# A four-layer image network on one core: rows padded to a half of the array, the middle convolution tile on TensorE, the second projection in two column tiles

## The chip, the cores and the metric

The kernel runs on one core of a Trainium2 chip. The metric is the device time in microseconds (us) from start to end of the program; lower is better. All work is in float32 but for two feed-forward layers in fp8.

## What is computed

Thirty-two images of 56 x 56 pixels and 24 channels pass through two convolution blocks, a linear attention with a feed-forward layer, and a Fourier mixing layer with another one. The convolution block is the part that the change is about:

```
rw  = sigmoid(mean(x) @ Wr + br)                    # routing weights of each image
h   = x . (sum_e rw_e Wpw_e) + bias                 # 24 -> 96 channels, per image
h   = relu(bn1(h))
h   = sum_e rw_e * depthwise3x3(h, Wdw_e)           # per image and channel
h   = relu(bn2(h))
h   = h . (sum_e rw_e Wpwl_e) + bias                # 96 -> 24 channels, per image
x   = bn3(h) + x
...
t = t + attention(ln(t));  t = t + ffn_fp8(ln(t))
t = t + ifft(relu(diag * fft(relu(bn(ln(t) @ w1))))) @ w2;  t = t + ffn_fp8(ln(t))
```

## The kernel before

**Tiling.** Four images go together in a group (the code calls it a quad), eight groups in all. A group's state `T` has 4 x 24 = 96 rows (partitions), row 24 i + c for channel c of image i, and 3136 columns (pixels). Three such tiles take turns, so up to three groups are under way. The 4 x 96 = 384 hidden channels of a convolution make NT = 3 tiles of 128 rows: tile 0 is image 0 and a third of image 1, tile 1 the rest of image 1 and two thirds of image 2, tile 2 the rest. The weights of the four images stand in one block-diagonal matrix: `Wk1` (96 rows x 384 columns) and `Wk2` (three times 128 rows x 96 columns). A picture is cut into NS = 4 strips of 14 rows.

**A convolution layer.** For each strip and each hidden tile, TensorE makes the hidden values in two pieces of seven or eight picture rows (`hidden`, line 647; 392 or 448 columns) in one PSUM bank, and ScalarE rectifies each piece into `H1` (line 1015) before TensorE may write the next. The nine taps of tiles 0 and 1 are VectorE's (`taps`, line 1347), eight operations of 784 columns on `acc`, with the centre tap on ScalarE (line 1023). The taps of the last tile, `TJ` = 2, are TensorE's (line 666): 36 matmuls with diagonal weights, in four tiles of 64 x 64. ScalarE rectifies both kinds (lines 1046, 1052). `conv_out` is the second projection: for tiles 0 and 1, four matmuls of 128 rows by 96 columns, two in each of two PSUM banks (line 681), then for the last tile four of 64 rows by 96 columns (line 687). VectorE adds the result to `T` (line 1363). A float32 matmul stands in the trace as two records, each with its own weight load.

**Other stages.** A *middle* stream (m in the tables; PSUM banks 3 and 4) does two layer norms, the attention and the first feed-forward layer; a *back* stream (b; banks 5 to 7) does two layer norms, the Fourier layer and the second feed-forward layer. In a layer norm, line 711 centres 448 columns with a full-array matmul and line 702 sums the squares in four tiles of 32 columns. Lines 622, 747, 924 and 946 are transposes. The Fourier layer's first matmuls (line 856) read `Y`, a view of `arena`, whose row 96 holds ones for the bias; GpSimd fills it, and two zero pads, for each group (line 604).

**The order.** Each engine runs four streams, c (convolution up to the taps), d (`conv_end`), m and b, merged in the order of a table of numbers, `TURNS`: "c7 m1" is seven steps of c and one of m. Within a stream the groups follow each other. Engines meet only through semaphores.

## Time and profile before

| | us |
|---|---|
| median of 3 runs | 2727.1 |
| lowest and highest | 2726.68, 2732.29 |
| the profiled execution | 2732.07 |
| its span, first to last instruction | 2730.1 |

The profile is of one execution. A busy time is the union of an engine's instructions; matmuls overlap in it, so a duration of one record is longer than its share of the stream, and the step from start to start of what follows is the better measure. PE is TensorE, PEld its weight loads, DVE VectorE, ACT ScalarE, POOL GpSimd. The mean granted clock of TensorE was 0.88 of full speed, that is, it stood at 2.4 GHz for most of the time and at 1.2 GHz for the rest.

### The profile page before, as it was taken

Reading aid. Unit: us, or ns where it says so; the run is one execution under the profiler, and the core shown is the slowest. Engines: PE = TensorE matmul, PEld = TensorE weight load, DVE = VectorE, ACT = ScalarE, POOL = GpSimd, SP = SyncE. Lnnn points to the kernel's source line nnn. Section 1 sums busy time; section 2 is a strip of 40 time slices with the busy share of each in tenths; the row PEclk is TensorE's granted clock in tenths of the full one; section 3 lists DMA queues with packets and bytes.
Section 4 is the critical chain, followed back from the end, with each engine's and each line's share of the span. In section 5 each row is a group of like instructions: output and inputs, shape, how many; then the busy total and the mean of one; then the engine's idle time right before and its main releaser. Section 6 shows DMA issues by size and latency. Waiting matters only on the chain.

```text
span 2730.1 us, 49134 instructions
## 1 busy us (share of the span) xinstructions
PE 2370.9 (87%) x19776; PEld 1324.3 (49%) x19776; DVE 1955.3 (72%) x3878; ACT 1680.7 (62%) x2818; POOL 69.3 (3%) x119
## 2 busy tenths in 40 slices
PE   3867979999898988989898989989899998987866
PEld 1323434564346634664346634665355634663562
DVE  4766778588775977678785978578786887755243
ACT  2324455756756666666756658666776667756644
POOL 1000000000000000000000000000000000000000
PEclk9878888989888988989898998989899998977865
DMA  4001000000001000010001000010000000000000
GB/s 131 1 1 18 1 1 1 11 10 1 18 1 19 2 1 19 2 19 1 13 6 20 1 1 19 2 19 1 1 19 9 2 1 19 2 1 1 19 1 18
DMA packets 108592, 29.43 MB, mean 11 GB/s; under 512 B 104144, under 2 KB 104272, under 8 KB 107984
## 3 DMA queue, kind: packets, MB, share of 16 engines
q1 hardware_dynamic: 108368, 26.29, 4.8%
q8 instruction: 159, 2.61, 0.4%
q14 instruction: 65, 0.53, 0.1%
HBM read 16.64 MB, written 9.63 MB: 10 GB/s over the span
## 4 chain that ended last, share of the span: by engine, by line
PE 61%; DVE 19%; ACT 14%; issue 4%; SPq 1%; DMA 0%; ACTq 0%; POOL 0%; DVEq 0%; POOLq 0%
PE P L666 13%; PE P L647 9%; PE P L711 6%; PE P L681 6%; DVE acc L1347 5%; PE P L856 4%; PE P L687 3%; PE P L702 2%; PE P L869 2%; PE P L897 2%; ACT H L1015 2%; PE P L911 2%; PE P L784 2%; DVE SQ L1482 2%; PE P L725 2%
## 5 line engine op out<-in xcount | busy, mean ns | idle before, releaser
L1347 DVE SCALAR_TENSOR_TENSOR acc<-H,Dm,acc 128x784 f32<-128x784 f32 x1024 | 989.6, 1026 | 189.6 <-ACT acc L1023 189.2
L647 PE MATMUL P<-T,Wk 96*128 96x448 f32 (+1 forms) x768 | 409.3, 618 | 68.4 <-ACT H L1015 51.6
L666 PE MATMUL P<-H,diag 64*64 64x392 f32 x4608 | 409.9, 506 | 5.6 <-DVE T L1363 4.8
L1015 ACT ACTIVATE H<-P,biasA 128x448 f32<-128x448 f32 (+1 forms) x384 | 238.6, 621 | 234.9 <-PE P L647 188.4
L666 PEld LDWEIGHTS P<-H,diag 64*64 64x64 f32 x4608 | 174.3, 137 | 223.3 <-issue 211.3
L711 PE MATMUL P<-T,pack_b 96*96 96x448 f32 x448 | 229.2, 600 | 12.0 <-DVE T L1363 5.8
L647 PEld LDWEIGHTS P<-T,Wk 96*128 96x128 f32 x768 | 137.1, 208 | 180.0 <-ACT H L1015 109.6
L681 PE MATMUL P<-acc,Wk 128*96 128x392 f32 x512 | 202.1, 542 | 25.3 <-ACT acc L1052 25.2
L1046 ACT ACTIVATE acc<-P,biasT 128x392 f32<-128x392 f32 x128 | 68.7, 583 | 228.7 <-PE P L666 228.7
L881 PE MATMUL P<-pack_b,arena 128*96 128x112 f32 x928 | 134.4, 302 | 41.1 <-DVE roots L1482 22.6
L881 PEld LDWEIGHTS P<-pack_b,arena 128*96 128x96 f32 x928 | 116.2, 193 | 72.9 <-DVE roots L1482 32.0
L681 PEld LDWEIGHTS P<-acc,Wk 128*96 128x96 f32 x512 | 87.6, 178 | 126.2 <-issue 125.7
L1023 ACT ACTIVATE acc<-H,Dm 128x784 f32<-128x784 f32 x128 | 121.4, 949 | 27.4 <-PE P L687 25.7
L1482 DVE SCALAR_TENSOR_TENSOR SQ<-P,fneg,arena 96x224 f32<-96x224 f32 x64 | 27.6, 431 | 133.6 <-ACT arena L1156 133.2
L1363 DVE SCALAR_TENSOR_TENSOR T<-P,bias,T 96x392 f32<-96x392 f32 x128 | 75.8, 618 | 65.3 <-PE P L687 61.3
L1052 ACT ACTIVATE acc<-acc,biasA 128x784 f32<-128x784 f32 x128 | 119.0, 950 | 5.2 <-DVE acc L1347 5.1
L856 PEld LDWEIGHTS P<-pack_b,arena 97*64 97x64 f32 x1792 | 111.9, 216 | 18.4 <-issue 10.4
L1116 ACT ACTIVATE mid<-P 128x448 f16<-128x448 f32 x168 | 91.8, 546 | 44.9 <-PE P L823 44.7
L856 PE MATMUL P<-pack_b,arena 97*64 97x96 f32 x1792 | 116.4, 292 | 1.7 <-DVE arena L1387 1.6
L1132 ACT ACTIVATE arena<-P 128x384 f32<-128x384 f32 x112 | 93.9, 854 | 35.9 <-PE P L856 29.5
L1156 ACT ACTIVATE arena<-P,pack_b 96x224 f32<-96x224 f32 (+1 forms) x128 | 59.7, 516 | 70.3 <-DVE arena L1466 68.1
L687 PE MATMUL P<-acc,Wk 64*96 64x392 f32 x256 | 100.3, 510 | 0.0
(186 smaller groups left out, 3886.3 us busy)
## 6 DMA issues: line engine op xcount, KB each, us to landing
xin<-in_x SPq DMA_DIRECT2D x224, 42.0 KB, 2.3
out_y<-arena SPq DMA_DIRECT2D x8, 1176.0 KB, 5.7
pack_b<-in_pack_b SPq DMA_DIRECT2D x1, 3804.0 KB, 17.3
arena<-in_pack_s SPq DMA_DIRECT2D x1, 1444.0 KB, 8.5
pack_a<-in_pack_a SPq DMA_DIRECT2D x1, 1084.0 KB, 5.3
pack_i<-in_pack_i SPq DMA_DIRECT2D x1, 318.0 KB, 3.1
arena<-in_pack_k SPq DMA_DIRECT2D x1, 192.0 KB, 3.2
```

The costliest lines, as they stand in the source:

```text
L647: pe.matmul(conv_rows(slice(0, 128), H1B, m), Wk1[:, 128 * (u % NT):128 * (u % NT + 1)], image_rows(T[q % 3], a + r0, m), start=True, stop ...
L666: last = pe.matmul(conv_rows(slice(64 * h, 64 * (h + 1)), CVB + r, HH), diag[64 * r:64 * (r + 1), tap, :], H1[64 * r:64 * (r + 1), slot(s, ...
L681: pe.matmul(conv_rows(slice(0, R), CVB + h, HH), Wk2[:, j, :], image_rows(acc[:, (NT * s + j) % N2, :], HH * h, HH), start=(j == 0), stop= ...
L687: last = pe.matmul(conv_rows(slice(0, R), CVB + h, HH), w, image_rows(acc[rows, (NT * s + TJ) % N2, :], HH * r, HH), start=False, stop=(r ...
L711: pe.matmul(P[0:R, norm.cen[c % NC], 0:CK], par["cen"][0:R, :], T[q % 3][:, CK * c:CK * (c + 1)], start=True, stop=True).then_inc(norm.cen ...
L856: last = pe.matmul(P[64 * j:64 * (j + 1), B0 + g % BN, R * s:R * (s + 1)], Y_x[:, 4 * g + s, :], par["fw1"][0:R + 1, R * j:R * (j + 1)], s ...
L881: last = pe.matmul(P[0:R, B0 + g % BN, o:o + 2 * HW], Y2[:, s // 2, s % 2, :], par["f"][:, s // 2, :], start=True, stop=True)
L1015: act.activation(H1[:, slot(s, j), o + r0:o + r0 + m, 1:1 + HW], conv_rows(slice(0, 128), H1B, m), ACT.Relu, bias=biasA[:, j, 1:2]).then_i ...
L1023: act.activation(acc[:, u % N2, :].rearrange("p (r w) -> p r w", w=HW), H1[:, slot(s, j), 1:1 + SR, 1:1 + HW], ACT.Copy, scale=Dm[:, j, CE ...
L1052: act.activation(a, a, ACT.Relu, bias=biasA[:, j, 0:1]).then_inc(h2_ready.sem, 1)
L1132: act.activation(Hf[:, :, 4 * g:4 * g + 4].rearrange("p c x -> p x c"), P[:, B0 + g % BN, 0:4 * R].rearrange("p (s n) -> p s n", s=4), ACT ...
L1347: ins = ve.scalar_tensor_tensor(a, H1[:, slot(s, j), r:r + SR, c:c + HW], Dm[:, j, tap:tap + 1], a, ALU.mult, ALU.add)
```

## The change

- Rows: 16 spare rows come first in `T` and all that is laid out like it, so R is 112 (`RC` is the old 96). Images 0 and 1 have rows 16 to 63, images 2 and 3 rows 64 to 111. Transposes to and from this layout, and results in it, are 112 rows or columns wide.
- `TJ` is 1: TensorE's taps take the middle hidden tile; VectorE's are tiles 0 and 2.
- `hidden` (now line 680): the pieces come in the order tile 0, 2, 1. Tile 0 needs only images 0 and 1 and contracts over rows 0 to 63; tile 2 contracts over rows 64 to 111; tile 1 over all 112.
- `conv_out`: first the middle tile's four matmuls (line 716), then, for each bank, tile 0 into output rows 0 to 63 and tile 2 into rows 64 to 111 (line 720), 128 rows by 64 and by 48 columns. They are as many as before: eight.
- GpSimd: the row of ones becomes a fill of 32 rows by 3136 columns (rows 96 to 127 of the arena), made before the third layer norm writes row 96 and up; ScalarE's first copy there waits for it. One more small fill comes before attention, and TensorE and ScalarE wait for both.
- The middle stream's first matmul of a group waits for VectorE's last addition of the group before (`added`) instead of ScalarE's copy (`out_half`).
- The turned tile of the Fourier layer is made in seven groups of four instead of six of up to five.
- One more VectorE operation in the setup, other constants, and new tables `TURNS`.

```diff
--- before.py
+++ after.py
@@ -27,7 +27,9 @@
 TOK = HW * HW
 CH = 24
 QI = 4
-R = QI * CH
+RC = QI * CH
+PAD = 64 - 2 * CH
+R = PAD + RC
...
-        Wk2 = sb("Wk2", [128, NT, R])
+        Wk2p = sb("Wk2", [128, PAD + NT * RC])
+        Wk2 = Wk2p[:, PAD:].rearrange("p (j n) -> p j n", j=NT)
...
-            return 4 if j == TJ else 2 * (s % 2) + j
+            return 4 if j == TJ else 2 * (s % 2) + j // 2
+
+        pieces = ((0, 0), (0, 1), (2, 0), (2, 1), (TJ, 0), (TJ, 1))
+        NP = len(pieces)
+
+        def piece_rows(s, k):
+
+            a, n, o = strip_rows(s)
+            return (a, 8, o) if k == 0 else (a + 8, n - 8, o + 8)
...
                 hold(pool_e, normM.y_ready, normM.y_ready.at(q, NCK))
-                pool_e.memset(YT[:, :, R:R + 1], 1.0).then_inc(ones_ready.sem, 1)
+                pool_e.memset(YT[:, :, RC:RC + 1], 1.0).then_inc(ones_ready.sem, 1)
+                pool_e.wait_ge(ones_ready.sem, ones_ready.at(q, 1))
+                pool_e.memset(bdw[2][:, 0:PAD], 0.0).then_inc(ones_ready.sem, 1)
 
             def back(q):
                 yield
 
                 if q == 0:
                     pool_e.wait_ge(setup_late.sem, 1)
+                hold(pool_e, normB.y_ready, normB.y_ready.at(q, 0))
+                pool_e.memset(arena[96:128, reg1:reg1 + TOK], 1.0).then_inc(fpads_set.sem, 1)
+                pool_e.wait_ge(fpads_set.sem, fpads_set.at(q, 1))
+                yield
                 hold(pool_e, out_stored, out_stored.at(q, 16))
-                for n, (dst, value) in enumerate(((Y[0:R, TOK:], 0.0), (Y[R:R + 1, :], 1.0), (Hf[:, :, HW:64], 0.0))):
-                    pool_e.memset(dst, value).then_inc(fpads_set.sem, 1)
-                    pool_e.wait_ge(fpads_set.sem, fpads_set.at(q, n + 1))
+                for n, dst in enumerate((arena[:, reg1 + TOK:reg1 + 64 * HW], Hf[:, :, HW:64])):
+                    pool_e.memset(dst, 0.0).then_inc(fpads_set.sem, 1)
+                    pool_e.wait_ge(fpads_set.sem, fpads_set.at(q, n + 2))
...
-                for u in range(NU):
-                    a, n, _ = strip_rows(u // NT)
-                    for k, (r0, m) in enumerate(((0, 8), (8, n - 8))):
+                for s in range(NS):
+                    for e, (j, k) in enumerate(pieces):
+                        a, n, _ = piece_rows(s, k)
                         yield
-                        if u == 0 and k == 0:
+                        if s == 0 and e == 0:
                             pe.wait_ge(cw_ready.sem, cw_ready.at(q, L + 1))
                         else:
-                            pe.wait_ge(h1_ready.sem, h1_ready.at(q, 2 * (L * NU + u) + k))
-                        pe.matmul(conv_rows(slice(0, 128), H1B, m), Wk1[:, 128 * (u % NT):128 * (u % NT + 1)],
-                                  image_rows(T[q % 3], a + r0, m), start=True, stop=True).then_inc(h1_psum.sem, 1)
+                            pe.wait_ge(h1_ready.sem, h1_ready.at(q, NP * (L * NS + s) + e))
+                        rows = {0: slice(0, 64), TJ: slice(0, R), 2: slice(64, R)}[j]
+                        pe.matmul(conv_rows(slice(0, 128), H1B, n), Wk1[rows, 128 * j:128 * (j + 1)],
+                                  image_rows(T[q % 3][rows, :], a, n), start=True, stop=True).then_inc(h1_psum.sem, 1)
...
-                pe.wait_ge(h2_ready.sem, h2_ready.at(q, L * NV + TJ * (s + 1)))
-                for j in range(TJ):
-                    for h in range(2):
-                        pe.matmul(conv_rows(slice(0, R), CVB + h, HH), Wk2[:, j, :], image_rows(acc[:, (NT * s + j) % N2, :], HH * h, HH),
-                                  start=(j == 0), stop=False)
+                pe.wait_ge(h2_ready.sem, h2_ready.at(q, L * NV + 2 * (s + 1)))
                 for r in range(2):
                     for h in range(2):
                         rows = slice(64 * h, 64 * (h + 1))
-                        w = Wk2[rows, TJ, :] if r == h else Wk2t[rows, :]
-                        last = pe.matmul(conv_rows(slice(0, R), CVB + h, HH), w,
-                                         image_rows(acc[rows, (NT * s + TJ) % N2, :], HH * r, HH), start=False, stop=(r == 1))
-                        if r == 1:
-                            last.then_inc(cv_psum.sem, 1)
+                        w = Wk2p[rows, TJ * RC:TJ * RC + R] if r == h else Wk2t[rows, :]
+                        pe.matmul(conv_rows(slice(0, R), CVB + h, HH), w,
+                                  image_rows(acc[rows, (NT * s + TJ) % N2, :], HH * r, HH), start=(r == 0), stop=False)
+                for h in range(2):
+                    for j, out_rows, w in ((0, slice(0, 64), Wk2p[:, 0:64]), (2, slice(64, R), Wk2[:, 2, 2 * CH:RC])):
+                        last = pe.matmul(conv_rows(out_rows, CVB + h, HH), w, image_rows(acc[:, (NT * s + j) % N2, :], HH * h, HH),
+                                         start=False, stop=True)
+                    last.then_inc(cv_psum.sem, 1)
...
-                    pe.wait_ge(ffns[0].out_half.sem, ffns[0].out_half.at(q, 0))
+                    pe.wait_ge(ffns[0].added.sem, ffns[0].added.at(q, 0))
...
-                    for xx in range(5 * g, min(5 * g + 5, HW // 2)):
-                        o = R * (xx % 5)
-                        last = pe.transpose(P[0:4 * K1, B0 + g % BN, o:o + R], Wf2[:, xx, :], par["ident"][0:R, 0:R])
+                    for xx in range(4 * g, 4 * g + 4):
+                        o = R * (xx % 4)
+                        last = pe.transpose(P[0:4 * K1, BB[g % BN], o:o + R], Wf2[:, xx, :], par["ident"][0:R, 0:R])
...
+                    if n == 2 and c == 0:
+                        act.wait_ge(fpads_set.sem, fpads_set.at(q, 1))
...
-        "d7 b1 c10 m1 c10 m1 c6 b1 c4 m1 c6 b1 c4 m1 c6 b1 c4 m1 c6 b1 c4 m1 c6 b1 c4 m1 c6 b1 c4 m1 b1 "
+        "d7 b2 c11 m1 c10 m1 c5 b1 c4 b1 c1 m1 c5 b1 c4 b1 c2 m1 c4 b1 c4 b1 c2 m1 c4 b1 c4 b1 c2 m1 c4 b1 c4 "
```

Line numbers shift: 647 to 680, 666 to 699, 687 to 716, 681 to 720, 711 to 743, 702 to 734, 604 to 628 and 633.

TensorE around the second projection of the first strip of the fourth group. Lines 911 and 924 are steps of the Fourier layer, 666 the taps. Before:

```order
L711 MATMUL P<-T,pack_b 96x448
L702 MATMUL P<-mid,pack_b 32x112 x4
L911 MATMUL P<-pack_b,arena 96x112 x5
L681 MATMUL P<-acc,Wk 96x392 x4
L687 MATMUL P<-acc,Wk 96x392
L687 MATMUL P<-acc,Wk2t 96x392 x2
L687 MATMUL P<-acc,Wk 96x392
L711 MATMUL P<-T,pack_b 96x448
L702 MATMUL P<-mid,pack_b 32x112 x4
L924 MATMUL P<-pack_i,arena 116x96 x28
L647 MATMUL P<-T,Wk 128x448
L666 MATMUL P<-H,diag 64x392 x36
```

Now, at the same projection (757 spreads the deviations of a layer norm):

```order
L680 MATMUL P<-T,Wk 128x448
L757 MATMUL P<-thirdsm,selb 112x448 x2
L716 MATMUL P<-acc,Wk 112x392
L716 MATMUL P<-acc,Wk2t 112x392 x2
L716 MATMUL P<-acc,Wk 112x392
L720 MATMUL P<-acc,Wk 64x392
L720 MATMUL P<-acc,Wk 48x392
L720 MATMUL P<-acc,Wk 64x392
L720 MATMUL P<-acc,Wk 48x392
L680 MATMUL P<-T,Wk 128x448
```

The four matmuls over 128 rows moved behind the four over 64 rows and are 64 and 48 columns wide, and the neighbours are other steps: the convolution stands earlier against the other streams.

TensorE in the hidden pieces of the fourth group's second layer. Before (823 and 809 are feed-forward matmuls, 946 output transposes):

```order
L823 MATMUL P<-mid,w1q 128x448 x2
L647 MATMUL P<-T,Wk 128x448
L946 MATMUL P<-pack_i,T 112x96 x12
L647 MATMUL P<-T,Wk 128x392
L823 MATMUL P<-mid,w1q 128x448
L809 MATMUL P<-mid,w2q 96x448 x3
L946 MATMUL P<-pack_i,T 112x96 x4
L647 MATMUL P<-T,Wk 128x448
```

Now:

```order
L743 MATMUL P<-T,pack_b 112x448
L680 MATMUL P<-T,Wk 128x448
L734 MATMUL P<-SQ,pack_b 32x112 x4
L743 MATMUL P<-T,pack_b 112x448
L734 MATMUL P<-SQ,pack_b 32x112 x4
L680 MATMUL P<-T,Wk 128x392
L743 MATMUL P<-T,pack_b 112x448
L734 MATMUL P<-mid,pack_b 32x112 x4
L680 MATMUL P<-T,Wk 128x448
```

As before, single pieces stand between steps of other streams; those of tiles 0 and 2 now use 64 x 128 tiles of the array, while line 743 and the feed-forward matmuls use all of it.

GpSimd around the fills for the second group. 567 and 590 build the diagonals, 573 and 596 clear edge rows. Before:

```order
L567 TENSOR_TENSOR diag<-pack_i,Dm 128x576 [waits edge_rows_zero_tensor,conv_weights_ready]
L604 MEMSET arena 96x448 [waits diagonals_ready,out_stored]
L604 MEMSET arena 1x3584 [waits fourier_pads_set]
L604 MEMSET arena 128x96x8 [waits fourier_pads_set]
L573 MEMSET H 128x2x56 [waits fourier_pads_set,acc_ready]
```

Now:

```order
L628 MEMSET arena 32x3136 [waits diagonals_ready,normalised_ready_back]
L596 MEMSET H 128x2x56 [waits fourier_pads_set,acc_ready]
L596 MEMSET H 128x56 [waits edge_rows_zero,taps_in_psum]
L596 MEMSET H 128x2x56 [waits edge_rows_zero_tensor,acc_ready]
L596 MEMSET H 128x56 [waits edge_rows_zero,taps_in_psum]
L633 MEMSET arena 128x448 [waits edge_rows_zero_tensor,out_stored]
L633 MEMSET arena 128x96x8 [waits fourier_pads_set]
```

The long fill stands ahead of a layer's four edge clears, the pads behind them.

## Rows read from the trace of the kernel before

In a timeline the columns are start and length in us, engine, line, operation, output and inputs, form and number of records. A form like 96\*128 is rows by columns of the weights.

**Rows 1.** Page: span, busy time of engines, chain shares by engine
```profile
span 2730.1 us, 49134 instructions
...
PE 2370.9 (87%) x19776; PEld 1324.3 (49%) x19776; DVE 1955.3 (72%) x3878; ACT 1680.7 (62%) x2818; POOL 69.3 (3%) x119
...
PE 61%; DVE 19%; ACT 14%; issue 4%; SPq 1%; DMA 0%; ACTq 0%; POOL 0%; DVEq 0%; POOLq 0%
```

**Rows 2.** Busy us by engine, granted clock, in start, middle and end
```profile
core 0: us, PE busy (x) PEld busy (x) DVE busy (x) ACT busy (x) POOL busy (x), PEclk, DMA share, GB/s
0.00:400.00 400.00, 295.93 (x1589) 126.19 (x1589) 261.18 (x455) 155.03 (x253) 15.15 (x27) 0.87 0.11 26
400.00:2400.00 2000.00, 1830.00 (x16074) 1039.64 (x16072) 1550.68 (x3037) 1341.98 (x2248) 49.75 (x89) 0.91 0.05 8
2400.00:2731.00 331.00, 244.93 (x2115) 158.48 (x2115) 143.48 (x388) 183.65 (x317) 4.40 (x4) 0.69 0.03 8
```

**Rows 3.** Chain that ended last: shares of the span by line
```profile
by line: PE P L666 12.6%; PE P L647 9.0%; PE P L711 6.5%; PE P L681 5.6%; DVE acc L1347 5.4%; issue 4.5%; PE P L856 4.2%; PE P L687 2.6%; PE P L702 2.2%; PE P L869 2.1%; PE P L897 2.1%; ACT H L1015 1.8%; PE P L911 1.6%; PE P L784 1.5%; DVE 
```

**Rows 4.** Timeline, TensorE, one second projection: start, us, line, form, records
```profile
928.01 2.80 PE L681 MATMUL P<-acc,Wk 128*96 128x392 f32 x8
930.74 0.57 PE L687 MATMUL P<-acc,Wk 64*96 64x392 f32 x1
...
931.80 0.49 PE L687 MATMUL P<-acc,Wk2t 64*96 64x392 f32 x1
...
932.23 0.99 PE L711 MATMUL P<-T,pack_b 96*96 96x448 f32 x2
933.15 0.40 PE L702 MATMUL P<-mid,pack_b 96*32 96x112 f32 x8
933.48 2.74 PE L924 MATMUL P<-pack_i,arena 96*116 96x96 f32 x28
```

**Rows 5.** Timeline, TensorE: full tiles between 32-column tiles
```profile
954.26 1.67 PE L711 MATMUL P<-T,pack_b 96*96 96x448 f32 x4
955.85 0.40 PE L702 MATMUL P<-mid,pack_b 96*32 96x112 f32 x8
956.18 1.02 PE L647 MATMUL P<-T,Wk 96*128 96x448 f32 x2
957.13 0.40 PE L702 MATMUL P<-SQ,pack_b 96*32 96x112 f32 x8
```

**Rows 6.** Groups of instructions on TensorE: busy us, mean ns, idle before
```profile
L666 PE MATMUL P<-H,diag 64*64 64x392 f32 x4608 | 409.9, 506 | 5.6 <-DVE T L1363 4.8 <-ACT H L1015 0.8
L647 PE MATMUL P<-T,Wk 96*128 96x448 f32 x576 | 308.4, 619 | 51.9 <-ACT H L1015 35.6 <-DVE biasT L1328 15.6
...
L681 PE MATMUL P<-acc,Wk 128*96 128x392 f32 x512 | 202.1, 542 | 25.3 <-ACT acc L1052 25.2
...
L869 PE MATMUL P<-pack_b,arena 128*64 128x58 f32 x3072 | 93.9, 223 | 1.0 <-ACT arena L1132 0.9
...
L747 PE MATMUL P<-pack_i,mid 96*112 96x96 f32 x224 | 38.5, 311 | 6.3 <-ACT mid L1079 4.2 <-POOL mid L595 2.1
...
L924 PE MATMUL P<-pack_i,arena 96*116 96x96 f32 x224 | 22.1, 250 | 1.1 <-ACT arena L1174 1.1
```

**Rows 7.** Waits of line 647: us in total, times, longest
```profile
PEld P L647 <- ACT H L1015: 109.6, 105, 2.7
```

**Rows 8.** Timeline, line 856 in two column tiles: matmuls and weight loads
```profile
2028.18 1.04 PEld L856 LDWEIGHTS P<-pack_b,arena 97*64 97x64 f32 x16 [0.65 <-issue]
2028.18 1.20 PE L856 MATMUL P<-pack_b,arena 97*64 97x96 f32 x16
...
2029.31 1.02 PE L647 MATMUL P<-T,Wk 96*128 96x448 f32 x2
```

**Rows 9.** Line 681: shortest, median and longest record
```profile
L681 PE MATMUL P<-acc,Wk x512: 490/492/941, 75.9 to 2390.7; 128*96 128x392 f32 x171
```

**Rows 10.** Line 604, the fills on GpSimd
```profile
L604 POOL MEMSET arena<- x24: 467/742/3096, 34.5 to 2547.0; 96x448 f32 x8, 1x3584 f32 x8, 128x768 f32 x8
```

More of the change, by code:

```diff
@@ L732, in gram @@
                         y = YT[:, BPG * (g % 2) + s, :]
-                        last = pe.matmul(P[0:R + 1, 4, 0:R + 1], y, y, start=(g == 0 and s == 0),
+                        last = pe.matmul(P[0:RC + 1, MB[1], 0:RC + 1], y, y, start=(g == 0 and s == 0),
                                          stop=(g == NCK - 1 and s == BPG - 1))
@@ L1038, in rectify_taps @@
+                        relu1(s, e)
+                        if k == 1 and j != TJ:
+                            yield
+                            centre_tap(s, j, e)
             def rectify_taps(q, L, s):
@@ L1579, in _parameters, with below @@
 def _parameters(a):
-    row_c = np.arange(R) % CH
+    row_c = np.concatenate([np.zeros(PAD, int), np.arange(RC) % CH])
+    com_c = row_c[PAD:]
     hid = np.arange(NT * 128) % HID
     p = {}
+    def below(v, ahead=0):
+        return np.pad(v, ((PAD, 0), (ahead, 0)))
     def tiles(v):
```

301 lines of the change are left out of this document (157 added, 144 removed), and 214 rows, old and new, of the table TURNS.

## The prediction

> **What bounds the kernel now.** I read the engines' busy times first. TensorE is busy 87% of the span, VectorE 72%, ScalarE 62%, and the chain of work that ended last runs through TensorE for 61% of it [rows 1]. By stage: between 400 and 2400 us TensorE is busy 1830 of 2000 us; in the first 400 us it is idle 104 us and in the last 331 us 86 us, because there few groups of images overlap [rows 2]. So a term is worth its full price only in the middle. The chain by line then says how much of a line's time is on the path: line 681 has 5.6% and line 687 2.6%, together 224 us of 2730; line 647 has 9.0%, 246 us [rows 3].
>
> **The second projection (the gain).** Before, one projection of a strip is eight records of line 681 (four float matmuls, two records each) and eight of line 687. The first eight start at 928.01 and line 687 starts at 930.74: 2.73 us. Line 687 takes until the next line starts at 932.23: 1.49 us. Together 4.22 us [rows 4]. In 2.73 us the engine streams 8 records of 392 columns, 0.33 us each (2.64), and 0.09 us are left, just where the tiling changes from the full array to two row tiles. Line 687 streams four rounds of two records that start in pairs (4 x 0.33 = 1.32); 0.17 us remain: 0.08 for the first weight load, which nothing hides, and 0.09 for leaving the tiling.
>
> After, line 716 is the old line 687 with 112 output rows, and line 720 has four matmuls in two column tiles, 64 and 48 wide. If each pair runs together, line 720 streams four rounds: 1.32, plus 0.06 for the first load (64 columns against 96 for 0.08) and 0.09 for leaving. With the entry into row tiles (0.09, formerly inside the 2.73) the new projection costs 0.09 + 1.49 + 1.32 + 0.15 = 3.05 us; I take 3.04. It saves 1.18 us; there are 64 strips (8 groups x 2 layers x 4), so 75.5 us. These are rows at the full clock of 2.4 GHz; the mean record of line 681 is 542 ns against a median of 492 [rows 6, 9], so some ran at the half clock and I multiply by 1.10: **83 us**. Of the old 64 x 4.22 = 270 us, 224 were on the chain, 83%. The gain on the path is **69 us**.
>
> Do the column pairs run together? The trace has such tiles. Line 666 has four 64x64 tiles with 392 columns: 4608 records in 409.9 us, 0.089 us each against 0.33 alone, nearly four at once [rows 6]. Line 869, two column tiles of 58 columns, takes 0.031 us a record where 58/392 x 0.33 gives 0.049 alone [rows 6]. Line 856 is the row against: 16 records of 96 columns from 2028.18 to 2029.31, 1.13 us, where perfect pairs would need 0.65; but its weight loads alone are busy 1.04 us, so loads bound it [rows 8]. At 392 columns a record streams 0.33 us over a load of 0.06. I take full pairing; the other end is a loss, priced below.
>
> The Trainium skill speaks less hopefully: in "TensorE: Matmul & The Clock Gate", Part 3, its table of measured speedups gives three column tiles 2.38 times, not 3. An estimate with that page's 0.79 would stretch the 1.32 us to 1.67 and take about 20 us from the gain; line 666 here shows no such loss.
>
> **The hidden matmuls (the cost).** The outer tiles' pieces at line 680 now contract over rows 0 to 63 or 64 to 111, so they run in 64x128 tiles, between neighbours that mostly use the full array. They gain nothing by it: each writes the one hidden bank and waits for the piece before. What a change of tiling costs is in a quiet stretch: line 711 takes four records from 954.26 to 955.85, 1.59 us, of which 4 x 0.377 (448 columns) is 1.51 and 0.08 to 0.09 is the exit to the 32-column tiles; line 647, between two such groups, takes 0.95 us for two records where 0.75 would do: 0.09 to leave and 0.11 for a weight load that is not hidden behind the matmul before it [rows 5]. So a change costs 0.09 plus 0.08 to 0.11: 0.19 us. Counted over the whole order of TensorE with each line's tile, there are 832 changes before and 1173 after. 64 of the 341 more are inside the projection and paid above; 277 remain, 277 x 0.19 = 53 us, 58 with the same clock factor. Where TensorE waits for ScalarE anyway the entry is free: 105 of 384 loads of line 647 did [rows 7], 27%, and entries are half of the changes, so 13% off: 50 us. Line 647 streams 288 x 0.75 + 96 x 0.66 = 279 us and has 246 on the chain, 88%. The cost on the path is **44 us**; its bounds are 0 (no drain for this tile) and 58.
>
> The Trainium skill has this rule, "TensorEngine Tiling (Array Packing)", section Tiling Modes: changing the mode, not merely the tile, drains the array. It gives no price; the trace agrees, with 0.09 us.
>
> **Wider rows.** Three transposes stream 112 columns instead of 96. At lines 747 and 924 that is 448 records [rows 6] of 16 more columns: 16/392 x 0.33 = 13 ns, 6 us; the output transposes, by the same step, up to 3 more. Loads of 112 columns after a change of tiling are 13 ns longer, some 250 times: 3 us. Together 9 to 12, on the path **8 us**. ScalarE's copies of the turned tile go from six to seven for each group of images, behind other work except in the last group, 1 us.
>
> **GpSimd and waits.** The long fill moves: 1x3584 took 3.10 us [rows 10], now 32x3136, by length 2.7 us, in front of ScalarE's first centred copy of the third layer norm. It only has to wait for the fourth layer norm of the group before, and a whole feed-forward stage follows that; GpSimd is busy 69 us of 2730 [rows 1]. I count nothing. If it stands behind an edge clear that waits for VectorE, all 2.7 us show, 8 times, 22 us at most. The second small fill before attention delays TensorE's first transpose, which already waited for that fill (2.1 us in all [rows 6]): 8 x 0.17, 1 us. The middle stream's first matmul now waits for VectorE's last addition, one operation later: 0 to 1 us each, I take 1 in all. VectorE's taps, the largest share outside TensorE, keep their number and size.
>
> **The sum.** -69 + 44 + 8 + 1 + 1 + 1 = -14 us. The order of all engines is also a new one. Before, 164 us of TensorE's work, by the row durations, lay behind the last projection; now 208: the convolutions run ahead. They start earlier (the third group's transposes after 261 us of such work instead of 319), which fills part of the 104 us idle at the start and takes work to the end. I take -6 for it, with bounds of -55 (some 30% of the 190 us idle at both ends) and +30 (the 44 us more at the end, run at two thirds). Sum **-20 us** on the profiled execution's 2732.1, so 2712; the median of the runs shown is 5 us lower, so **2707 us**.
>
> **Rivals.**
> - The changes of tiling win (slower). The saved time is on the path only while TensorE is what ends last at the projection; the changes are paid in every stretch. If half of the 83 us is off the path (VectorE's taps or the single hidden bank set the pace) and the 58 us are paid in full, with 11 for widths and waits: -41 + 58 + 11 = +28, 2755. It decides once less than (50 + 11)/83 = 73% of the gain is on the path; the chain says 83%. 24%.
> - The new order wins more: -14 - 45 = -59, 2668. For it: 190 us of idle at both ends [rows 2]. Against it: no row says the new order fills them. 17%.
> - The 64x128 tiles drain nothing, so the change of the hidden pieces is free: -69 + 10 = -59, 2668. Against: line 687 paid 0.17 us in the same tile [rows 4]. 7%.
> - The change doesn't do what it says: column pairs run one after another. Line 720 then takes 2.64 and a projection 4.37: +10 us, and with 44 + 11 + 0: +65, 2792. Only line 856 speaks for it. 4%.
>
> **How the numbers follow.** My forecast has 48% and its own range is 2685 to 2730. The range reaches to both kinds of neighbour: 2648 to 2760. A measurement tells 0.2%, 5.5 us, from no change. Faster: 0.48 x 0.78 + 0.17 + 0.07 = 0.61. Same: 0.48 x 0.18 + 0.04 of the first rival = 0.13. Slower 0.26.
>
> **What would show it.** Line 720's records start in pairs 0.33 us apart and its eight take 1.4 to 1.5 us (right), or one by one for 2.7 (wrong). Line 680's pieces of 64 rows take 0.95 us and the line behind them starts 0.09 late. TensorE's time at lines 716 and 720 on the chain falls from 8.2% to 5.5 to 6% of the span. Line 647's share, 9.0%, rises to 10 to 11% at line 680. ScalarE shows no wait for GpSimd at the third layer norm. I am wrong if the chain's share of VectorE rises while TensorE's idle time between 400 and 2400 us, 170 us now, grows by more than 40 us.

## The result and the profile after

| | before | after |
|---|---|---|
| median | 2730.7 us | 2757.5 us |
| lowest and highest of 6 runs | 2726.7, 2732.5 | 2748.2, 2766.2 |
| the profiled span | 2730.1 | 2752.3 |

The ratio is 1.01 (95%: 1.0078 to 1.0122): the changed kernel is slower, by 27 us. The forecast was 2707 us, with 61% on faster. The sign was wrong; the time lies inside the range, near the 2755 of the first rival.

The page of the changed kernel, as [rows 1] (busy time and instructions of each engine, then the chain by engine):

```profile
span 2752.3 us, 49178 instructions
...
PE 2350.1 (85%) x19776; PEld 1284.7 (47%) x19776; DVE 1951.9 (71%) x3879; ACT 1679.9 (61%) x2826; POOL 70.1 (3%) x130
...
PE 62%; DVE 16%; ACT 14%; issue 5%; SPq 3%; DMA 1%; ACTq 0%; DVEq 0%
```

TensorE is busy 21 us less than before, yet the span is 22 us longer. The chain has a new part: SyncE's queue (SPq) with 3% where it had 1%, and DMA with 1% where it had 0%.

The same three stretches as [rows 2] (columns as there):

```profile
0.00:400.00 400.00, 287.24 (x1574) 120.06 (x1575) 264.13 (x453) 149.94 (x246) 15.47 (x31) 0.84 0.11 26
400.00:2400.00 2000.00, 1806.27 (x15494) 984.04 (x15494) 1524.87 (x2990) 1317.44 (x2215) 49.99 (x94) 0.90 0.04 8
2400.00:2753.00 353.00, 256.58 (x2713) 180.64 (x2711) 162.85 (x437) 212.55 (x366) 4.67 (x5) 0.79 0.03 8
```

TensorE's idle time is 113, 194 and 96 us, where it was 104, 170 and 86. In the middle 2000 us it gets through 15494 matmuls where it did 16074, and those missing turn up behind 2400 us (2713 against 2115, in a stretch 22 us longer).

The chain by line, as [rows 3] (680 was 647, 716 was 687, 720 was 681):

```profile
by line: PE P L699 12.4%; PE P L680 11.0%; PE P L743 6.0%; issue 4.6%; PE P L888 4.4%; PE P L716 4.3%; DVE acc L1381 4.1%; PE P L720 3.4%; PE P L901 2.8%; SPq L553 2.5%; PE P L734 1.9%; PE P L929 1.8%; ACT H L1047 1.8%; PE P L913 1.8%; DVE 
```

The hidden matmuls rose from 9.0% to 11.0%, as forecast. Lines 716 and 720 have 7.7%; 5.5 to 6 were forecast, 8.2 stood before. And line 553, SyncE's input load, has 2.5% of the chain, where all of SyncE's queue had 1% before.

One second projection of the changed kernel, TensorE's timeline (start, length, line, form, records), as [rows 4]:

```profile
566.96 1.02 PE L680 MATMUL P<-T,Wk 48*128 48x448 f32 x2
567.91 0.59 PE L757 MATMUL P<-thirdsm,selb 96*112 96x448 bf16 x2
568.42 0.58 PE L716 MATMUL P<-acc,Wk 64*112 64x392 f32 x1
...
569.93 1.53 PE L720 MATMUL P<-acc,Wk 128*64 128x392 f32 x8
571.39 1.01 PE L913 MATMUL P<-pack_b,arena 128*96 128x112 f32 x8
```

Line 716 takes 1.51 us from its start to that of line 720, and line 720's eight records 1.46: together 2.97, where the sum had 1.49 and 1.32 + 0.15. The column pairs stream two at a time, as forecast, and the 48-row piece of line 680 takes the 0.95 us that was forecast.

What was not forecast is before the first step of each group. Groups of TensorE's instructions at the input transposes (busy, mean ns, idle before and its releasers), before and then after:

```profile
L622 PE MATMUL P<-pack_i,xin 112*96 112x112 f32 x224 | 37.8, 321 | 27.3 <-DMA xin<-in_x 27.3
```
```profile
L655 PE MATMUL P<-pack_i,xin 112*112 112x112 f32 x224 | 41.6, 335 | 75.8 <-DMA xin<-in_x 75.8
```

TensorE waits 76 us for input data where it waited 27. The diff of the kernel has one line on this that the prediction did not look at:

```diff
                     n = q * NCK + g
                     if n >= XG:
-                        sp.wait_ge(in_tp.sem, n - XG + 1)
-                    o = RC * BPG * (n % XG)
+                        sp.wait_ge(in_tp.sem, n - XG + 2)
+                    o = PAD + RC * BPG * (n % XG)
```

The input buffer has `XG` = 4 slots for the seven blocks of a group. A transpose of 112 columns also reads the 16 columns ahead of its slot, which are the end of the slot before it. So a slot may be filled again only when the next slot has been read too, and the load waits for one block more. The loads of the next group's first four blocks are issued ahead of time; the fourth of them (block 3 of group q + 1) now waits until that group's own first block is transposed. SyncE works in order, and behind this load stand the store of group q - 2 and the other loads. SyncE's queue in the kernel before, and after:

```profile
736.37 0.33 SPq L536 DMA_DIRECT2D out_y<-arena  x1
850.03 15.46 SPq L531 DMA_DIRECT2D xin<-in_x  x28
1046.31 0.33 SPq L536 DMA_DIRECT2D out_y<-arena  x1
```
```profile
807.98 0.49 SPq L558 DMA_DIRECT2D out_y<-arena  x1
808.51 319.85 SPq L553 DMA_DIRECT2D xin<-in_x  x28
1128.40 0.52 SPq L558 DMA_DIRECT2D out_y<-arena  x1
```

Before, the store left at 1046 and the loads for the next group followed when slots came free. After, the store leaves at 1128, behind the last of 28 loads, which were begun at 808. What happens there, in the timeline of all engines (the number in brackets is the idle time before a record):

```profile
1125.85 1.33 PE L655 MATMUL P<-pack_i,xin 112*112 112x112 f32 x12
...
1126.44 1.91 SPq L553 DMA_DIRECT2D xin<-in_x  x4
...
1128.40 0.52 SPq L558 DMA_DIRECT2D out_y<-arena  x1
...
1128.96 14.02 SPq L553 DMA_DIRECT2D xin<-in_x  x22
...
1130.35 0.92 PE L655 MATMUL P<-pack_i,xin 112*112 112x112 f32 x4 [2.14 <-DMA xin<-in_x]
...
1135.47 1.00 PE L655 MATMUL P<-pack_i,xin 112*112 112x112 f32 x4 [4.19 <-DMA xin<-in_x]
```

The first transposes free the load (1126.44), the store goes out behind it, and the rest of the loads follow in single file while TensorE waits for each: 2.14 us, 4.19 us, at the head of a group on which all its other engines depend.

### The profile page after: what moved, and what is told of

The parts are those of the page before. It is cut to its first block, busy times and chain, and to the rows that moved or that the text cites. A ratio compares the mean times of both kernels' runs of the same rounds, so it can differ in the third digit from the quotient of the medians.

```text
span 2752.3 us, 49178 instructions
## 1 busy us (share of the span) xinstructions
PE 2350.1 (85%) x19776; PEld 1284.7 (47%) x19776; DVE 1951.9 (71%) x3879; ACT 1679.9 (61%) x2826; POOL 70.1 (3%) x130
## 4 chain that ended last, share of the span: by engine, by line
PE 62%; DVE 16%; ACT 14%; issue 5%; SPq 3%; DMA 1%; ACTq 0%; DVEq 0%
PE P L699 12%; PE P L680 11%; PE P L743 6%; PE P L888 4%; PE P L716 4%; DVE acc L1381 4%; PE P L720 3%; PE P L901 3%; SPq L553 2%; PE P L734 2%; PE P L929 2%; ACT H L1047 2%; PE P L913 2%; DVE SQ L1517 2%; PE P L757 2%
## 5 line engine op out<-in xcount | busy, mean ns | idle before, releaser
L680 PE MATMUL P<-T,Wk 64*128 64x448 f32 (+5 forms) x768 | 432.8, 648 | 72.8 <-ACT H L1047 46.0
L743 PE MATMUL P<-T,pack_b 112*112 112x448 f32 x448 | 237.2, 621 | 19.7 <-ACT mid L1094 10.3
L680 PEld LDWEIGHTS P<-T,Wk 64*128 64x128 f32 (+2 forms) x768 | 129.5, 208 | 224.2 <-ACT H L1047 119.7
L716 PE MATMUL P<-acc,Wk 64*112 64x392 f32 x256 | 132.9, 650 | 29.8 <-ACT acc L1083 29.7
L888 PEld LDWEIGHTS P<-pack_b,arena 113*64 113x64 f32 x1792 | 117.0, 216 | 41.6 <-issue 25.2
L716 PE MATMUL P<-acc,Wk2t 64*112 64x392 f32 x256 | 131.3, 653 | 0.0
L888 PE MATMUL P<-pack_b,arena 113*64 113x96 f32 x1792 | 126.9, 304 | 3.6 <-ACT arena L1165 2.7
L1397 DVE SCALAR_TENSOR_TENSOR T<-P,bias,T 112x392 f32<-112x392 f32 x128 | 78.6, 623 | 64.2 <-PE P L720 63.1
L743 PEld LDWEIGHTS P<-T,pack_b 112*112 112x112 f32 x448 | 69.3, 188 | 88.8 <-issue 71.4
L720 PE MATMUL P<-acc,Wk 128*64 128x392 f32 (+1 forms) x512 | 110.6, 558 | 0.0
L655 PE MATMUL P<-pack_i,xin 112*112 112x112 f32 x224 | 41.6, 335 | 75.8 <-DMA xin<-in_x 75.8
```

What stands on the lines that cost most here:

```text
L680: pe.matmul(conv_rows(slice(0, 128), H1B, n), Wk1[rows, 128 * j:128 * (j + 1)], image_rows(T[q % 3][rows, :], a, n), start=True, stop=True ...
L716: pe.matmul(conv_rows(slice(0, R), CVB + h, HH), w, image_rows(acc[rows, (NT * s + TJ) % N2, :], HH * r, HH), start=(r == 0), stop=False)
L720: last = pe.matmul(conv_rows(out_rows, CVB + h, HH), w, image_rows(acc[:, (NT * s + j) % N2, :], HH * h, HH), start=False, stop=True)
L743: pe.matmul(P[0:R, norm.cen[c % NC], 0:CK], par["cen"][0:R, :], T[q % 3][:, CK * c:CK * (c + 1)], start=True, stop=True).then_inc(norm.cen ...
L888: last = pe.matmul(P[64 * j:64 * (j + 1), BB[g % BN], RC * s:RC * (s + 1)], Y_x[:, 4 * g + s, :], par["fw1"][0:R + 1, RC * j:RC * (j + 1)] ...
```

## The experiments

Each ratio is to the kernel before, measured on the same chip, with its 95% interval. Medians of the kernel before were 2736.0, 2731.9 and 2730.6 us on the three chips, so differences of medians between kernels on different chips are good to some 5 us; where it matters the difference of the two ratios is given too, in us of the kernel before. With the intervals of both ratios such a difference is known to some 8 to 13 us. "Best" is the name, in the labels and here, of the kernel with both edits of the first three experiments.

**The input wait, taken away in the changed kernel.** Each slot gets 16 zero columns of its own, and the load waits as it did before.

```diff
-        xin = sb("xin", [BLK, PAD + XG * BPG * RC])
+        SL = PAD + BPG * RC
+        xin = sb("xin", [BLK, XG * SL])
...
-                        sp.wait_ge(in_tp.sem, n - XG + 2)
-                    o = PAD + RC * BPG * (n % XG)
+                        sp.wait_ge(in_tp.sem, n - XG + 1)
+                    o = PAD + SL * (n % XG)
...
-                        o = RC * (BPG * (n % XG) + s)
+                        o = SL * (n % XG) + RC * s
```

> The changed kernel, with 16 zero columns of its own in front of each of the four input slots, so that a slot may be loaded again as soon as its own transposes are done (the wait of the kernel before). In the changed kernel TensorE is idle 70 us before its input transposes (line 655), in the kernel before 21 us (line 622). Theory A (the stricter wait on the input slots is the missing cost): that idle time falls back to 15 to 30 us and the time by 35 to 50 us, to 2708 to 2722 us (before: 2731). Theory B (the changes of the array's tiling at the hidden matmuls are the whole of the slowdown, the input wait is covered by other slack): 2745 to 2758, and the idle time turns up at another line.

2735.3 us (10 runs, 2724.9 to 2744.5), ratio 1.0001 (0.998 to 1.0021): 22 us less than the changed kernel's 2757.5 (27 by the ratios), and no different from the kernel before. That is below theory B's range, and a smaller fall than theory A's 35 to 50: the wait is a cost, but not all of it. The input transposes now wait:

```profile
L656 PE MATMUL P<-pack_i,xin 112*112 112x112 f32 x224 | 38.3, 316 | 51.6 <-DMA xin<-in_x 51.1 <-ACT T L1029 0.4
```

So 24 of the 76 us went, and 22 to 27 us of the end with them. The other 24 us over the 27.3 of before stay, although the wait is the old one.

**The row tiles of the hidden matmuls, taken away.** All pieces contract over 112 rows with the full array (their weights are zero in the rows of images that the tile does not hold); the rest is the changed kernel. TensorE's order then has 900 changes of tiling, not 1173.

```diff
-                        rows = {0: slice(0, 64), TJ: slice(0, R), 2: slice(64, R)}[j]
-                        pe.matmul(conv_rows(slice(0, 128), H1B, n), Wk1[rows, 128 * j:128 * (j + 1)],
-                                  image_rows(T[q % 3][rows, :], a, n), start=True, stop=True).then_inc(h1_psum.sem, 1)
+                        pe.matmul(conv_rows(slice(0, 128), H1B, n), Wk1[:, 128 * j:128 * (j + 1)],
+                                  image_rows(T[q % 3], a, n), start=True, stop=True).then_inc(h1_psum.sem, 1)
```

> The changed kernel with all hidden matmuls over all 112 rows (the weights outside an image are zero), so that they use the full array; the input wait stays as in the changed kernel. Theory B: the 277 more changes of tiling go, the hidden matmuls' share of TensorE's time falls from 399 us to about 370, and the time falls by 35 to 50 us, to 2708 to 2722. Theory A: the time falls only by what the hidden matmuls' charge fell, up to 29 us, 2728 to 2745, and the idle time before the input transposes stays at 70 us. If row tiles cost nothing: 2757.

2701.6 us, ratio 0.9878 (0.9855 to 0.9901). This one edit turns the change from slower to faster than before: 56 us (61 by the ratios) for 273 changes of tiling, 0.20 us each, more than theory B's 35 to 50. The granted clock is 0.892 against 0.875.

**Both edits.**

> Both edits: own zero columns for each input slot, and hidden matmuls on the full array. If both costs are real and add up, 2757 - 45 - 35 = 2670 to 2685 us, 2% under the kernel before. If they hide behind one another (either alone gives all), 2705 to 2722.

2660.4 us (4 runs, 2656.7 to 2661.6), ratio 0.9725 (0.9699 to 0.9751). That beats both kernels: 70 us under the one before (76 on this chip), 97 under the changed one, and it is below the 2670 to 2685 that were expected. The two causes seem to be worth more together than apart: the row tiles 75 us (2735.3 to 2660.4, 0.27 us per change of tiling), the input wait 41 us (2701.6 to 2660.4). By the ratios that is 14 us more than apart, which is just clear of its interval of some 13. Its page and its chain by line:

```profile
PE 2264.9 (85%) x19776; PEld 1275.4 (48%) x19776; DVE 1948.1 (73%) x3879; ACT 1677.6 (63%) x2826; POOL 70.2 (3%) x130
...
PE 55%; DVE 23%; ACT 14%; issue 5%; SPq 2%; DMA 1%; ACTq 0%; DVEq 0%
```
```profile
by line: PE P L699 10.8%; PE P L680 8.5%; DVE acc L1381 8.3%; PE P L743 6.1%; issue 5.3%; PE P L888 4.4%; PE P L716 3.3%; PE P L901 2.9%; PE P L720 2.7%; DVE SQ L1517 2.1%; PE P L734 1.9%; ACT H L1047 1.9%; PE P L929 1.9%; SPq L554 1.7%; PE
```

Lines 716 and 720 now have 6.0% of the chain, what the prediction expected of the changed kernel, and VectorE's taps (line 1381) have 8.3%, twice the 4.1% they had there: with TensorE relieved, more of the path is VectorE's.

**The same suspect, put into the kernel before.** Tile 0's pieces contract over rows 0 to 47 there, in a row tile. Tile 0 holds only hidden units of images 0 and 1, so nothing of the computation is left out, and number and columns of all matmuls stay. 186 changes of tiling are added.

```diff
-                        pe.matmul(conv_rows(slice(0, 128), H1B, m), Wk1[:, 128 * (u % NT):128 * (u % NT + 1)],
-                                  image_rows(T[q % 3], a + r0, m), start=True, stop=True).then_inc(h1_psum.sem, 1)
+                        rows = slice(0, 2 * CH) if u % NT == 0 else slice(0, R)
+                        pe.matmul(conv_rows(slice(0, 128), H1B, m), Wk1[rows, 128 * (u % NT):128 * (u % NT + 1)],
+                                  image_rows(T[q % 3][rows, :], a + r0, m), start=True, stop=True).then_inc(h1_psum.sem, 1)
```

> The kernel before with one edit: the hidden matmuls of tile 0 (images 0 and 1) contract over rows 0 to 47 alone, where the other rows' weights are zero, so that 128 of the 384 pieces use a 64x128 tile. Counted over TensorE's order that makes 1018 changes of tiling instead of 832. Theory B (a change costs 0.19 us, more where it also brings the half clock): 186 x 0.19 to 0.26 = +35 to +48 us, 2765 to 2780 (before: 2731 to 2736). If the loss of the changed kernel came from its order and not from the tiles, this one, in the old order, stays within 8 us of before.

2771.2 us, ratio 1.0147 (1.012 to 1.0174): 39 us for 186 changes, 0.21 us each, in an order in which nothing else was touched, and within theory B's range. Its groups at the hidden matmuls (busy, mean ns), the full pieces and those in row tiles:

```profile
L648 PE MATMUL P<-T,Wk 96*128 96x448 f32 x384 | 209.2, 629 | 27.2 <-ACT H L1016 26.9
L648 PE MATMUL P<-T,Wk 48*128 48x448 f32 x192 | 111.5, 665 | 22.8 <-DVE biasT L1329 15.0 <-ACT H L1016 7.8
```

The pieces in row tiles contract over half the rows and take longer, 665 ns against 629 (619 for all of them before, [rows 6]). These means mix records at both levels of the clock.

**The column pairs, taken out of the best kernel.** The outer tiles' second projection uses the full array again, 128 rows by 112 columns, as many matmuls as before the change.

```diff
-                    for j, out_rows, w in ((0, slice(0, 64), Wk2p[:, 0:64]), (2, slice(64, R), Wk2[:, 2, 2 * CH:RC])):
-                        last = pe.matmul(conv_rows(out_rows, CVB + h, HH), w, image_rows(acc[:, (NT * s + j) % N2, :], HH * h, HH),
-                                         start=False, stop=True)
+                    for j in (0, 2):
+                        last = pe.matmul(conv_rows(slice(0, R), CVB + h, HH), Wk2p[:, j * RC:j * RC + R], image_rows(acc[:, (NT * s + j) % N2, :], HH * h, HH),
+                                         start=False, stop=(j == 2))
```

> The fastest kernel so far (own zero columns for the input slots, hidden matmuls on the full array, median 2660) with the outer tiles' second projection back on the full array, 128 rows by 112 columns, one matmul after another; 846 changes of tiling instead of 900. If the column pairs run together and are worth what the prediction took (64 x 1.3 us less 64 changes x 0.19, times 1.1): +75 to +85 us, 2735 to 2745. By the measured charges of lines 681 and 687, 294 us against 237: +50 to +62 us, 2710 to 2722. If pairs are worth nothing: 2650 to 2665.

2730.2 us (10 runs), ratio 0.9993 (0.9974 to 1.0013), against 2660.4: the pairs are worth 70 us at the end, 1.09 us per strip (73 by the ratios), between the two ranges expected. The groups of line 720 on the full array, and in pairs in the best kernel:

```profile
L720 PE MATMUL P<-acc,Wk 128*112 128x392 f32 x512 | 194.6, 525 | 0.0
```
```profile
L720 PE MATMUL P<-acc,Wk 128*64 128x392 f32 x256 | 104.6, 533 | 0.0
L720 PE MATMUL P<-acc,Wk 128*48 128x392 f32 x256 | 103.7, 530 | 0.0
```

The two groups of the pairs lie on top of each other, record for record as long as the full one.

**The new order on the old instructions.** The kernel before with the tables `TURNS` of the changed one, and four empty steps where the changed kernel has steps that the old one lacks.

```diff
+            def input_transposes(q):
+                if first(q):
+                    yield
...
-        "d7 b1 c10 m1 c10 m1 c6 b1 c4 m1 c6 b1 c4 m1 c6 b1 c4 m1 c6 b1 c4 m1 c6 b1 c4 m1 c6 b1 c4 m1 b1 "
+        "d7 b2 c11 m1 c10 m1 c5 b1 c4 b1 c1 m1 c5 b1 c4 b1 c2 m1 c4 b1 c4 b1 c2 m1 c4 b1 c4 b1 c2 m1 c4 b1 c4 "
```

> The kernel before, all its instructions and waits as they were, merged by the changed kernel's tables (empty steps where the changed kernel has one more). Theory C (the new order itself is worse): slower than before by 15 us or more, 2745 to 2770. If the order is neutral or better, as the prediction took: 2705 to 2735. Theories A and B say nothing of it, but need it not to be the whole of the 27 us.

2802.4 us, ratio 1.0247 (1.0215 to 1.0279): 66 us slower than the kernel before on its chip, with the same instructions and 848 changes of tiling against 832: worse than all that was expected. Its span and granted clock, and the input transposes:

```profile
core 0: 2807.9 us, clock 0.860
```
```profile
L630 PE MATMUL P<-pack_i,xin 112*96 112x112 f32 x224 | 37.0, 309 | 51.1 <-DMA xin<-in_x 49.8 <-DVE T L1373 0.4 <-ACT T L1005 0.3
```

The 24 us of input wait that `a_own_pads` had left are here too: they belong to the new order. Over all of TensorE, though, the idle time grew by 14 us only; 64 us are slower streaming (the table further down; the clock is 0.860, it was 0.880). The profiled execution is the slowest of the four.

**The old order on the new instructions.** The best kernel with the tables of the kernel before; the seventh turned group shares the step of the sixth, the step added at the input transposes is gone, and GpSimd's new step gets a turn.

```diff
                 for g in range(NTR):
-                    yield
+                    if g < NTR - 1:
+                        yield
```

> The fastest kernel so far (own zero columns, hidden matmuls on the full array), merged by the tables of the kernel before: the seventh turned group shares the sixth's step, and GpSimd's long fill stands directly before the two pads. Theory C (the new order is worse in itself, as it was by 67 us on the old instructions): faster than 2660 by 20 us or more, 2600 to 2640. Theory D (each order fits the instructions it was made for): 2655 to 2700.

2689.4 us, ratio 0.9846 (0.982 to 0.9871): 29 us slower than with the new tables (33 by the ratios), as theory D has it. So the new order is neither good nor bad in itself. It costs 66 us with the old instructions and gives 29 with the new ones. Why, no run shows.

**The stricter input wait in the kernel before.** The load waits for one block more, and the store goes ahead of the load that is now held up.

```diff
-                        sp.wait_ge(in_tp.sem, n - XG + 1)
+                        sp.wait_ge(in_tp.sem, n - XG + 2)
...
-                    load(q + 1, range(XG))
+                    load(q + 1, range(XG - 1))
                 if q >= 2:
                     store(q - 2)
+                if q + 1 < NQ:
+                    load(q + 1, range(XG - 1, XG))
```

> The kernel before with the changed kernel's stricter wait on the input slots (a slot is loaded again only when the next slot's transposes are done too); the stores of results are put ahead of the fourth load of the next group, so that they do not stand behind it. Theory A (this wait costs TensorE its idle time in any order): idle before line 622 rises from 21 to 40 to 60 us, time +15 to +30 us, 2746 to 2766. If the new order makes the wait dear (transposes of three groups in a row at once): within 8 us of before.

2733.9 us (10 runs), ratio 1.0009 (0.9987 to 1.003). TensorE's wait for input grows, and the end does not move:

```profile
L624 PE MATMUL P<-pack_i,xin 112*96 112x112 f32 x224 | 39.4, 324 | 40.8 <-DMA xin<-in_x 40.8
```

The old order has room for these 13 us more. The store behind the held load was not tried in this order.

**The changed kernel again, and with the store ahead of the held load.** The first has no edit and gives the spread between chips; the second has the same move of the store as above, with the stricter wait kept.

> The changed kernel, timed on the chip of the next two, so that all three stand side by side. Both theories: 2750 to 2765, ratio to before 1.008 to 1.012.

> The changed kernel with its stricter wait on the input slots kept, but the store of a finished group put ahead of the fourth load of the next group in SyncE's queue (in the changed kernel it stands behind that load, which now waits for the next group's first transposes: the trace shows the store of the first group at 808 us, in the kernel before at 736). If the input loss is the late store, whose transfer runs between the loads that TensorE waits for: 2728 to 2740, and the idle time before line 655 falls from 70 to about 50 us. If it is the fourth load, issued only when TensorE is already at the transposes: no more than 8 us faster, 2749 to 2760, idle 62 to 72.

> The same with hidden matmuls on the full array (2702 us without the moved store, 2660 with own zero columns). Late store: 2660 to 2675. Fourth load: 2692 to 2704.

The changed kernel took 2763.0 us (4 runs, 2758.9 to 2773.9), ratio 1.0123 (1.0093 to 1.0152). With the store ahead of the load it took 2752.3 (2749.7 to 2760.8), ratio 1.0085 (1.0067 to 1.0103), and with full hidden pieces as well 2685.8 (2672.3 to 2697.9), ratio 0.9834 (0.9798 to 0.987). So of the input wait's price the queue behind it is 11 us of 22 to 28 in the changed kernel, and 16 us (12 by the ratios) of 41 with full hidden pieces. With four runs each, the first is known to some 10 us and the second to some 12: that the store has a part is likely, how large it is stays open. Neither time lies where the late store alone or the held load alone would have put it. The input transposes' idle time falls with the move from 75.8 to 62.2 us, which is the held load's range:

```profile
L657 PE MATMUL P<-pack_i,xin 112*112 112x112 f32 x224 | 42.9, 344 | 62.2 <-DMA xin<-in_x 62.0
```

## Where the time went

The two kernels are joined by steps that were each measured (medians; by the ratios the differences are -42, -33, +75 and +27 to +33):

| step | median | difference |
|---|---|---|
| the kernel before | 2731 | |
| new instructions in the old order, own pads, full hidden pieces | 2689 | -42 |
| the new order | 2660 | -29 |
| the row tiles of the hidden pieces | 2735 | +75 |
| the stricter input wait with the store behind it | 2757 to 2763 | +22 to +28 |

How much of this is the clock? The granted clock of a profile says how long TensorE stood at the lower of its two levels, 1.2 GHz instead of 2.4: with 0.880 it is 24% of the span. For each kernel the table gives that time, and my sum over TensorE's records of the time from one start to the next, less the idle time that the trace shows between them ("charge"; over all lines it is the busy time of the page). The last column is the charge with the part that ran at 1.2 GHz, by the trace's own record of the clock, counted by half: an estimate of what the streaming would take at 2.4 GHz.

| kernel | at 1.2 GHz | charge | hidden line | both projection lines | idle | charge, at 2.4 GHz |
|---|---|---|---|---|---|---|
| before | 655 us | 2371 | 370 | 294 | 346 | 2110 |
| changed | 688 | 2350 | 399 | 237 | 390 | 2075 |
| a_own_pads | 653 | 2347 | 397 | 232 | 363 | 2078 |
| best | 521 | 2265 | 363 | 216 | 382 | 2060 |
| best_proj_full | 525 | 2344 | 360 | 302 | 375 | 2135 |
| best_old_order | 575 | 2269 | 364 | 204 | 407 | 2053 |
| b_first_tile_rows | 719 | 2416 | 394 | 295 | 339 | 2125 |
| b_new_order | 786 | 2435 | 390 | 310 | 361 | 2104 |

In b_new_order the charge is 64 us larger than before with the same instructions, and at 2.4 GHz it would be 6 us smaller. So the lower clock is the whole of the larger charge. The row tiles' price splits the same way: from a_own_pads to the best kernel the charge falls by 82 us, of which 64 are the clock, and 18 us are left for 273 changes, 0.07 us each. In b_first_tile_rows 45 us are 30 by the clock and 15 for 186 changes, 0.08 each. That is nearly the 0.09 which the rows of before showed for the drain at a change of tiling [rows 4, 5]. The pairs are another matter: from best_proj_full to best the clock stays (0.904 and 0.902), and of the 79 us by which the charge falls 75 are there at 2.4 GHz too.

That the clock costs this much shows within one kernel: the changed one took 2748.2 us at 0.879 and 2766.2 at 0.872, with identical instructions, 18 us for some 43 us more at 1.2 GHz. But a table of single executions is not one of medians. The profiled execution of a_own_pads was the fastest of its ten (0.880, their mean is 0.873), that of b_new_order the slowest of its four (0.860, mean 0.866). By the mean clocks on one chip, 0.873 and 0.903, taking the row tiles away saves 181 us at 1.2 GHz; with TensorE busy in 80% of them, half of that is 72 of the 75 us. The order adds 76 us at 1.2 GHz (0.876 and 0.866), at a busy share of 84% some 32 of its 66 us; the rest is not located.

## The prediction, point by point

The gain held. Two steps failed and made the sign wrong: SyncE's stricter wait was not counted at all (22 to 28 us), and a change of tiling was priced without its effect on the clock (44 us taken, 56 to 75 measured). The wider rows were sized too small as well.

**The gain of the column pairs: right.** 83 us of TensorE's time and 69 on the path were forecast. Between best_proj_full and best it is 86 on the two lines (302 to 216), 79 in all of TensorE, and 70 at the end, or 73 by the ratios, which is known to some 9 us; that 69 was met to a us is luck. The step by which pairs run fully together held. The estimate from the page "TensorE: Matmul & The Clock Gate" of the Trainium skill, Part 3, would have taken 20 us off; these rows, with two column tiles of 392 columns, show no such loss. At 2.4 GHz the two lines fell from 272 us before to 189 in the changed kernel and in the best, by 83 where 75.5 were forecast. As they ran in the changed kernel they fell by only 56 us (294 to 237), because 41% of their time was at 1.2 GHz there and 14% before. Most of that is line 716, which is now the first of the projection: 54% of its time, where line 687, behind line 681, had 1%.

**The price of the row tiles: too small, and mostly by another route.** The term was +44, with 58 as its upper bound. Measured: 56 in the changed kernel, 75 once the input wait is gone, 39 for 186 changes in the old order. The count of the changes was right (277 forecast, 273 undone). The step that failed is "a change costs 0.09 plus 0.08 to 0.11: 0.19 us" with 10% for the lower clock as a fixed surcharge. At the end a change costs 0.20 to 0.27 us. But at 2.4 GHz it costs TensorE only 0.07 us, 18 us for 273 changes where 53 were forecast: that leaves room for the drain, but hardly for the weight load that nothing hides. The larger part is the clock, which moves with the change: taking the row tiles away raised it from 0.873 to 0.903. The rule of the Trainium skill in "TensorEngine Tiling (Array Packing)", Tiling Modes, that a change of mode drains the array, spoke against this change, and the runs agree with it, by 0.07 to 0.09 us a change.

**The input wait: missed.** The added waits of GpSimd, ScalarE and TensorE were each priced; SyncE's stands in none of the steps, and its line is not in the diff as shown ahead. It costs 22 to 28 us in the changed kernel (41 with full hidden pieces), about as much as the whole loss. The method was at hand: a changed constant in a wait has to be followed to what is queued behind it. The view that shows it is SyncE's timeline, where the store moves from 1046 to 1128 us. What the wait costs could not have been read from the kernel before alone: in the old order, with the store ahead of the held load, it is worth nothing (+2 us, within the interval).

**The new order: wrong as a term.** -6 was taken, with bounds of -55 and +30. An order has no price of its own: +66 on the old instructions, -29 on the new ones. The second value lies within the bounds. My reason, that the start fills better, is not what the trace shows: TensorE's idle time in the first 400 us grew from 104 to 113 us, and with the instructions of the best kernel it is 116 us in the new order and 118 in the old. Part of the cost has a place, the 24 us more of input wait that come with the order.

**Widths, waits, fills: too small, or beside it.** 8 + 1 + 1 + 1 = 11 us were taken. The joined steps leave more: new instructions in the old order give -42, and with the pairs' -70 that leaves 28. This assumes that the pairs are worth the same in both orders, which was not measured. TensorE's own work accounts for most of it: outside the hidden pieces and the projections its charge at 2.4 GHz is 1531 us in best_old_order and 1508 before, 23 us more. The three wider transposes are 9 of them, as forecast; 4 are the centring matmuls of the layer norms (line 711 before), whose weights also grew from 96 to 112 columns (3 were taken for all longer weight loads); the rest is spread over other lines. The long fill costs nothing that shows: there is no wait of ScalarE for GpSimd in the changed trace.

**The sum.** -69 + 44 + 11 - 6 = -20 became -70 + 75 + 28 - 29 + 25 = +29, where 25 is the middle of the input wait's 22 to 28. 31 us of the miss are the row tiles, 25 the input wait, 17 the widths, and the order gave 23 back. By the ratios the same steps are -73 + 75 + 31 - 33 and 27 to 33.

**The rivals.** The first, that changes of tiling win, gave 2755 and the time is 2757.5, but not by its route: it had half of the gain off the path, and the gain was whole. The second, that the new order wins more, is right in sign and hidden by the rest. That the 64x128 tiles drain nothing, and that column pairs run one by one, are both refuted.

**What would show it.** Pairs in 1.46 us: right. Pieces of 64 rows in 0.95 us: right. Line 680 at 10 to 11% of the chain: right, 11.0. Lines 716 and 720 at 5.5 to 6%: wrong in the changed kernel (7.7), right in the best (6.0). VectorE's share fell from 19 to 16%, and the idle time in the middle grew by 24 us, not 40: neither sign of the failure that I had named came, since it came from elsewhere.

## What to carry to other kernels

Follow each changed constant in a wait to the queue it stands in, the DMA issuing one above all: a load that waits a step longer holds up every store and load behind it. A step that neither gains from a smaller tile nor runs beside another should keep its neighbours' tiling; here the whole loss and more came from pieces that had been given a row tile without need, and undoing that together with the input wait made a loss of 27 us a gain of 70. An order that helps one set of instructions can hurt another (-29 and +66 us here); where both change, measure the parts with each order before crediting either. And a price read at the full clock is not the price at the end where the edit moves the clock: compare the granted clocks of all executions, not of the two profiled ones.

## What the runs showed of the chip beyond that

A change of tiling costs more at the end than between its neighbours: 0.20, 0.21 and 0.27 us in three pairs of kernels, where TensorE's own price is 0.07 to 0.09. The granted clock moves along, by the mean of all executions on one chip: 0.878 to 0.869 with 186 changes more, 0.873 to 0.903 with 273 fewer. Even the order alone moves it, 0.876 to 0.866 with the same matmuls. Whether the drains lower the clock, or the waits that come with them, no run here tells apart.
